# Folding the first layer normalisation into the projection weights, with the x statistics taken late

## The reference

```python
x = x + gnn(layernorm(x), adj, W, a)      # first stage
x = x + ffn(layernorm(x), ...)            # second stage

def layernorm(x): return (x - mean) / sqrt(var + 1e-5)

def gnn(h, adj, W, a):
    Wh = h @ W
    e = (Wh @ a1)[:, :, None] + (Wh @ a2)[:, None, :]
    e = where(e > 0, e, 0.2 * e) + log(adj + 1e-6)
    return softmax(e) @ Wh

def ffn(x, ...):
    w = softmax(mean(x, axis=0) @ Wr + br)       # mean over the 128 graphs
    # per expert: two linear layers with batch norm and relu, one linear layer,
    # weighted by w and summed
```

## Time and profile before

| | us |
|---|---|
| median of 3 runs | 2536.35 (2535.84 to 2540.9) |
| the profiled execution | 2537.31 |
| its span | 2535.5 |
| PE busy | 2412.7 (95%) |
| DVE busy | 1717.1 (68%) |
| ScalarE busy | 1638.9 (65%) |
| POOL busy | 459.4 (18%) |

### The profile page before, as it was taken

How to read it: one execution, slowest core, us unless ns; L and a number is a source line. 1 busy time by engine, 2 the same in 40 slices (tenths; PEclk the granted TensorE clock), 3 DMA queues, 4 the chain that set the end, 5 groups by cost and what they waited for, 6 DMA issues and landing times.

```text
span 2535.5 us, 45093 instructions
## 1 busy us (share of the span) xinstructions
PE 2412.7 (95%) x16304; PEld 2218.3 (87%) x16304; DVE 1717.1 (68%) x2444; ACT 1638.9 (65%) x2497; POOL 459.4 (18%) x487
## 2 busy tenths in 40 slices
PE   6777776999999999999999999999999999999999
PEld 5666665999999999999999999999999999999998
DVE  4777775666666666666666666666666666666665
ACT  4666654666666666666666666666666666666665
POOL 3566553111011111111111111111100111011110
PEclk9999997999999999999999999999999999999999
DMA  3555552000000000000000000000000000000000
GB/s 125 172 186 173 179 165 67 26 20 22 25 17 17 25 25 25 25 25 25 25 25 25 25 25 25 25 25 25 25 25 25 25 24 17 25 17 19 21 17 26
DMA packets 91178, 116.16 MB, mean 46 GB/s; under 512 B 4700, under 2 KB 78856, under 8 KB 91144
## 3 DMA queue, kind: packets, MB, share of 16 engines
q1 hardware_dynamic: 91144, 115.73, 13.9%
HBM read 82.16 MB, written 33.55 MB: 46 GB/s over the span
## 4 chain that ended last, share of the span: by engine, by line
PE 83%; DVE 1%; ACT 0%; issue 0%; ACTq 0%; DVEq 0%
PE ps_y L1182 29%; PE ps_wide L171 28%; PE ps_wide L1164 25%; PE ps_t L132 1%; DVE h_lo L1069 0%; DVE h L1076 0%; PE ps_y L1230 0%; DVE z L1062 0%; DVE x1t L124 0%; ACT h_hi L971 0%; DVE feat_sum L1102 0%; ACT v L976 0%; DVE resb L179 0%; DVE z L1052 0%; DVE h_lo L1084 0%
## 5 line engine op out<-in xcount | busy, mean ns | idle before, releaser
L976 ACT ACTIVATE v<-ps_wide,bn_cols 128x256 f32<-128x256 f32 x768 | 434.3, 566 | 399.3 <-PE ps_wide L1164 269.9
L984 ACT ACTIVATE h<-ps_wide,bn_cols 128x512 f32<-128x512 f32 x512 | 399.0, 779 | 327.5 <-PE ps_wide L171 327.5
L1182 PE MATMUL ps_y<-wo_lo,h_hi 128*128 128x256 f32 x2048 | 579.1, 283 | 0.0
L1182 PE MATMUL ps_y<-wo_hi,h_hi 128*128 128x256 f32 x2048 | 577.4, 282 | 1.6 <-DVE h_lo L1084 1.6
L1182 PE MATMUL ps_y<-wo_hi,h_lo 128*128 128x256 f32 x2048 | 578.6, 283 | 0.0
L1164 PE MATMUL ps_wide<-xq_hi,wq_hi 128*128 128x256 f32 x1792 | 506.2, 282 | 14.9 <-PEq L185 9.2
L1164 PE MATMUL ps_wide<-xq_lo,wq_hi 128*128 128x256 f32 x1792 | 509.7, 284 | 0.0
L1164 PE MATMUL ps_wide<-xq_hi,wq_lo 128*128 128x256 f32 x1792 | 507.1, 283 | 0.0
L1084 DVE TENSOR_TENSOR h_lo<-h,h_hi 128x1024 fp32r<-128x1024 f32 x256 | 318.2, 1243 | 238.9 <-ACT h_hi L990 238.9
L1062 DVE SCALAR_TENSOR_TENSOR z<-ps_wide,bn_cols,v 128x512 f32<-128x512 f32 x256 | 192.2, 751 | 318.0 <-PE ps_wide L1164 318.0
L171 PE MATMUL ps_wide<-h_hi,w_hi 128*128 128x512 f32 x1024 | 404.3, 395 | 2.1 <-DVE h_lo L1069 2.1
(11 more groups left out here) (131 smaller groups left out, 3118.9 us busy)
## 6 DMA issues: line engine op xcount, KB each, us to landing
x_sb<-in_x SPq DMA_DIRECT2D x32, 512.0 KB, 3.9
res<-in_x SPq DMA_DIRECT2D x32, 512.0 KB, 5.8
x1t<-x_scratch SPq DMA_DIRECT2D x32, 512.0 KB, 3.3
resb<-x_scratch SPq DMA_DIRECT2D x32, 512.0 KB, 3.3
out<-resb SPq DMA_DIRECT2D x32, 512.0 KB, 3.0
adj_sb<-in_adj SPq DMA_DIRECT2D x32, 256.0 KB, 6.0
x_scratch<-h SPq DMA_DIRECT2D x16, 512.0 KB, 4.7
x_scratch<-w_bc SPq DMA_DIRECT2D x16, 512.0 KB, 4.5
```

What stands on the lines that cost most here:

```text
L976: nc.scalar.activation(v[:, slot, :], ps_l1[:, 0, 0:H], ACT.Identity, bias=bn_cols[:, 1, cols], scale=bn_cols[:, 0, cols]).then_inc(done, 1)
L984: nc.scalar.activation(h2[:, m, :], ps_l2[:, m, :], ACT.Relu, bias=bn_cols[:, 3, cols], scale=bn_cols[:, 2, cols]).then_inc(r2_done, 1)
L1182: mm = nc.tensor.matmul(ps_y[:, b4, :], h[:, c, cols], w[:, e, c, :], start=(e == 0 and k == 0 and b4 % per_bank == 0), stop=(e == E - 1 a ...
```

## The change

The mean is taken out by the weights: (x - mean) W equals x (W - column mean of W), so at the start two matmuls with a constant matrix of 1/256 (`mean_w`) give the column means and DVE subtracts them from `gw`. The division by the standard deviation is a scale for each row of Wh, and is given to the copy of ps_wide, which becomes one instruction per graph with `rstd1` as its scale. The normalised x isn't written any more: PE transposes `x_sb` itself, and the load of x two groups on waits for those transposes and for the statistics. The statistics of x are needed only by the time of the wh copy, so DVE takes them for g+1, behind the x1 sums, and POOL computes rstd1 behind the running sum. DVE accumulates one graph (`LB = 1`), POOL three. DVE's order in a step changes throughout.

```diff
-                    wait(sp, xn_done, num(g) - 1)
+                    wait(sp, xnT_ready, num(g) - 1)
+                    wait(sp, bnst1, num(g) - 1)
                     sp.dma_start(x_sb[p][:, :, :], x_g[num(g)]).then_inc(x_loaded[p], 16)
...
                 def rstd_1(g):
                     p = g[1]
                     pool.wait_ge(stats1_done, num(g) + 1)
-                    wait(pool, nb1_done, num(g))
-                    nc.gpsimd.tensor_tensor(ve1[:, :], mv1[p][:, :, 1], eps_cols[:, :], ALU.add)
-                    nc.gpsimd.tensor_tensor(neg_mean1[:, :], mv1[p][:, :, 0], minus_one[:, :],
-                                            ALU.mult).then_inc(ve1_done, 1)
+                    wait(pool, rstd1_done, num(g))
+                    nc.gpsimd.tensor_tensor(ve1[:, :], mv1[p][:, :, 1], eps_cols[:, :],
+                                            ALU.add).then_inc(ve1_done, 1)
                     pool.wait_ge(ve1_done, num(g) + 1)
+                    wait(pool, wh_copied, num(g) - 1)
...
-                nxt = ago(g, -2)
-                    if exists(nxt):
-                        rstd_1(nxt)
...
-                        nc.gpsimd.tensor_tensor(acc[:, HB:, :], acc[:, HB:, :], x1s_high[:, :, :],
+                        nc.gpsimd.tensor_tensor(acc[:, LB:, :], acc[:, LB:, :], x1s_high[:, :, :],
                                                 ALU.add).then_inc(acc_high_done, 1)
+                    nxt = ago(g, -1)
+                    if exists(nxt):
+                        rstd_1(nxt)
...
-                    for b4 in range(GB):
-                        last = nc.scalar.activation(xn[:, b4, :], x_sb[p][:, b4, :], ACT.Identity,
-                                                    bias=nb1[p][:, b4:b4 + 1], scale=rstd1[p][:, b4:b4 + 1])
-                    last.then_inc(xn_done, 1)
...
+                        act.wait_ge(rstd1_done, num(g) + 1)
                         wait(act, h_ready, num(g) - 1)
-                        nc.scalar.activation(wh[p][:, :, :], ps_wide[:, :, 0:D + 2], ACT.Copy).then_inc(wh_copied, 1)
+                        for b4 in range(GB):
+                            last = nc.scalar.activation(wh[p][:, b4, :], ps_wide[:, b4, 0:D + 2], ACT.Copy,
+                                                        scale=rstd1[p][:, b4:b4 + 1])
+                        last.then_inc(wh_copied, 1)
...
+                nc.vector.tensor_tensor(gw[:, :, 0:D], gw[:, :, 0:D], ps_wide[:, 0:1, 0:D].to_broadcast([P, C, D]),
+                                        ALU.subtract).then_inc(gw_centred, 1)
...
+                    if exists(nxt):
+                        wait(dve, rstd1_done, num(nxt) - 1)
+                        stats_1(nxt, 0)
+                        stats_1(nxt, 1)
                     if exists(a):
                         dve.wait_ge(e_done, num(a) + 1)
...
+                for c in range(C):
+                    last = nc.tensor.matmul(ps_wide[:, 0, 0:D], mean_w[:, :], gw[:, c, 0:D], start=(c == 0),
+                                            stop=(c == C - 1))
+                last.then_inc(col_mean_ready, 1)
+                pe.wait_ge(gw_centred, 1)
...
-                        pe.wait_ge(xn_done, num(nxt) + 1)
+                        pe.wait_ge(x_loaded[nxt[1]], 16 * (nxt[0] + 1))
...
-                                                           xn[:, b4, c * P:(c + 1) * P], ident[:, :])
+                                                           x_sb[nxt[1]][:, b4, c * P:(c + 1) * P], ident[:, :])
```

More of the change, by code:

```diff
@@ L299, in over_groups @@
             def over_groups(eng, step):
-                for i in range(-2, 2 * K0):
+                for i in range(-1, 2 * K0):
                     step((i // 2, i % 2), 0)
@@ L591, in aggregate_2, with add_part @@
                     last.then_inc(stats2_done, 1)
+                dve.wait_ge(col_mean_ready, 1)
+                nc.vector.tensor_tensor(gw[:, :, 0:D], gw[:, :, 0:D], ps_wide[:, 0:1, 0:D].to_broadcast([P, C, D]),
+                                        ALU.subtract).then_inc(gw_centred, 1)
                 def step(g, layer):
-                    p = g[1]
                     a = ago(g, 1)
+                    b = ago(g, 2)
+                    t = ago(g, 3)
+                    h = ago(g, 4)
                     r = a[1]
-                    nxt = ago(g, -2)
-                    def stats_part(b4):
-                        if exists(nxt):
-                            stats_1(nxt, b4)
+                    q = b[1]
+                    nxt = ago(g, -1)
+                    with_acc = exists(h) and not is_step(h, G - 2) and not is_step(h, G - 1)
+                    with_stats = exists(b) and not is_step(b, G - 1)
+                    def add_part(b4):
+                        if not with_acc or b4 >= LB:
+                            return
+                        if b4 == 0:
+                            dve.wait_ge(rstd2_done, num(h) + 1)
+                            dve.wait_ge(acc_low_done, num(h) + 1)
+                            dve.wait_ge(mean2_done, num(h) + 1)
+                        part = nc.vector.scalar_tensor_tensor(out=acc[:, b4, :], in0=x1[h[1]][:, b4, :],
+                                                              scalar=rstd_all[:, num(h), b4:b4 + 1],
+                                                              in1=acc[:, b4, :], op0=ALU.mult, op1=ALU.add)
+                        if b4 == LB - 1:
+                            part.then_inc(acc_low_done, 1)
+                    if exists(b):
+                        dve.wait_ge(rowsum_done, num(b) + 1)
+                    if exists(t):
+                        dve.wait_ge(bnst2, num(t) + 1)
                     if exists(a):
-                        stats_part(0)
                         dve.wait_ge(s_done, num(a) + 1)
@@ L611, in step @@
                                                        op1=ALU.max).then_inc(l_done, 1)
-                        stats_part(1)
+                    if exists(b):
+                        nc.vector.reciprocal(rinv[:, :], rowsum[:, :]).then_inc(rinv_done, 1)
+                    if exists(t):
+                        aggregate_2(t)
+                    add_part(0)
+                    if exists(a):
                         dve.wait_ge(l_done, num(a) + 1)
@@ L669, in step @@
                         last.then_inc(x1_done, 1)
-                    with_stats = exists(b) and not is_step(b, G - 1)
+                    if exists(nxt):
+                        wait(dve, rstd1_done, num(nxt) - 1)
+                        stats_1(nxt, 0)
+                        stats_1(nxt, 1)
                     if exists(a):
                         dve.wait_ge(e_done, num(a) + 1)
-                        if with_stats:
-                            stats_2(b, 0)
                         dve.wait_ge(adj_loaded[r], 16 * (a[0] + 1))
@@ L681, in step @@
                                                        op1=ALU.mult).then_inc(p_done, 1)
-                        if with_stats:
-                            stats_2(b, 1)
+                    if exists(nxt):
+                        stats_1(nxt, 2)
+                        stats_1(nxt, 3)
+                    if with_stats:
+                        stats_2(b, 0)
+                    if exists(nxt):
+                        dve.wait_ge(bnst1, num(nxt) + 1)
+                    if exists(a):
                         dve.wait_ge(p_done, num(a) + 1)
@@ L686, in step @@
                         nc.vector.tensor_reduce(rowsum[:, :], p_sb[:, :, :], AX_X, ALU.add).then_inc(rowsum_done, 1)
+                    if exists(nxt):
+                        aggregate_1(nxt)
                     if with_stats:
-                        for b4 in range(2 if exists(a) else 0, GB):
+                        for b4 in range(1, GB):
                             stats_2(b, b4)
```

64 lines of the change are left out of this document (13 added, 51 removed).

## The result

The changed kernel took 2514.85 us (median of four runs, 2514.15 to 2515.95), the kernel before 2536.19 beside it. The ratio is 0.9912, 95% interval 0.9895 to 0.9929: faster by 0.9%, 21 us. The direction is as forecast, the size isn't: 2529 was predicted, and the range ended at 2517.

The account below looks back on a forecast made before the run. A loop of waits in the first stage was taken as the bound: 31 x 10.48 = 324.9, + 4.3 + 7.2 = 336.4 against 344.4, so -8.0, + 1.0 = -7.0 us, giving 2529 against the 2536.35 median; range 2517 to 2541.

Parts of the forecast that it names:

- W: Time of ScalarE's four scaled wh copies in one step: forecast 1.55 us, bounds 1.18 and 1.96.
- The loop: First-stage cycle wh, ps_s, s_sb, xnT, projection, ps_h matmuls, next wh: 10.48 us a step after the change, from 10.82.
- The wait for x beside the loop: DVE's wait for x_sb, 2.15 us in one step, was held to be no gain in itself.
- POOL's hold on DVE: While POOL runs, DVE instructions with two SBUF inputs slow: l_sb takes 2.39 us beside wq_lo, its like 0.68.
- So res becomes a new wait of DVE, 1.2 us: In each step res lands 10.8 us after a wh start; the x1 sums would start at 9.56.
- The eight steps with wq_lo (4.3): DVE's accumulation waits behind POOL's wq_lo, delaying wh by 0.54 us in eight steps: 4.3 us.
- My 21.5 for wh: When wh starts in a step with wq_lo: 21.5 us, not the 20.96 due after two intervals.
- The six clock falls (7.2): PE's clock falls in six of the longer-waiting steps, slowing ps_s and transposes by 1.2 us each: 7.2 us.
- a choice between none and one in every step: No row shows PE's single pause of 1.70 us, so its falls were priced between these two extremes.
- Start: Column-mean matmuls and subtraction ahead of the first transposes, 2.7 us in place of the first xn: +0.5 us.
- End: p_sb held by POOL's longer multiply at the end: +0.5 us.
- neither the hold nor falls: Rival: res lands a microsecond sooner, accumulation precedes wq_lo, one or two falls; -17 us, 2519; chance 0.13.

Follow-up runs that it names:

- experiment 5: Changed kernel with a second pointer operand, a zero bias, on each of the four wh copies: 2537.00 us, ratio 0.9996.
- experiment 7: Changed kernel with wh copied by one unscaled instruction, the division by the standard deviation left out: 2506.43 us, ratio 0.9876.
- experiment 2: Kernel before, with the x statistics taken from the always-present gwT so DVE doesn't wait for x: 2534.56 us, ratio 0.9987.
- experiment 8: Changed kernel with PE's transposes of x put ahead of ps_s and ScalarE's xnT ahead of s_sb: 2485.01 us, ratio 0.9790.
- Experiment 6: Changed kernel with SP issuing the res load one step later: 2538.12 us, ratio 1.0002.
- experiment 3: Changed kernel with the x statistics taken two groups ahead, at the head of DVE's step: 2567.35 us, ratio 1.0119.

## Why the prediction was wrong

**What held.** W: 1.57 against 1.55; experiments 5 and 7 give 0.37 more and 0.54 less in W, and 0.38 more and 0.54 less in the loop. An estimate from the figures of the Trainium skill (ScalarE: Activation LUTs, What ACT_TABLE_LOAD costs) was 1.70; the row of s_sb was the better guide. The loop: 10.51 against 10.48, and link by link in the step shown no start is more than 0.05 off. The wait for x beside the loop: experiment 2. POOL's hold on DVE: 2.32 for the accumulation beside wq_lo. The Trainium skill (GPSIMD Engine Reference, Specifications and Key points) names for it instructions with two SBUF inputs, beside those in a 2-port perf mode, and the trace agrees: the x1 sums, one input from PSUM, take 1.66 at 229.55 though POOL's multiply starts at 229.42, while p_sb takes 2.06 in experiment 8.

**The step that failed** is "So res becomes a new wait of DVE, 1.2 us". The issue at 3.8 + 1.2 (5.1 to 5.4 measured in most steps) and the 5.8 to land are nearly right; what they were set against isn't. The x load that SP issues behind the transposes of x(g) is that of step g of its own program, but PE takes those transposes in its step g-1. The res that follows it in the queue is for group g-1, and DVE adds it at the end of the next interval, not of this one. In numbers, from the timeline of SP in the changed kernel and the landing of its res loads (us, min/median/max):

```profile
214.51 0.38 SPq L353 DMA_DIRECT2D res<-in_x  x1
```

```profile
DMA to landing us min/median/max: 4.4/5.7/6.6
```

That load lands at about 220.2, and the sums that use it start at 229.55, 9.3 later. It is 1.2 too late only for the sums one step ahead, and those are the ones in my working. Experiment 6 puts the load where the working had it, and the wait is there, at 1.9 instead of 1.2. Even with it the forecast would have been 7 us too low.

**What hung on it.** The eight steps with wq_lo (4.3): DVE's chain now starts 1.2 sooner, with PE at 9.56. My 21.5 for wh becomes 20.3, inside the 20.96. Measured in the step shown: neg_m ends at 228.58, the exponentials at 229.90, and wh has 0.17 to spare. That the spare is so small is shown by experiment 7. The six clock falls (7.2) were put in the steps that would wait longer, with a pause of 2.2. Those steps are no longer than the others, so the pause stays at 1.75, and no fall comes. The link from pause to fall was not wrong: at 2.03 and 2.11 there are eight (experiment 5). But that 1.7 brings no fall was a choice between none and one in every step, and came true without a row that said so. Two readings behind it were also off. The work around the one pause isn't unbroken, since PE waits 0.83 for xnT in each step. And ahead of the eight falls of before the pause for wh wasn't always about 1.2: it was 1.43 three times and 2.22 once.

**Mis-sized terms.** Start: +0.5 was forecast, and the first projection does start 0.4 later (16.32 against 15.95). But the first wh comes 1.1 earlier, since that projection ran in 5.23 instead of 6.71. The change isn't shown to be the cause: experiment 6 has the same instructions within 0.1 us of the same times up to there, and its first projection takes 6.68; over all the runs it is 5.2 to 6.7. The granted clock reads 1.00 there in either case, so it doesn't explain it. These 1.5 us are luck as far as is known. The first interval: my sum took 31 full ones, but the first has no ps_h matmuls and lasts 8.73, 1.75 less. (The 344.4 of before, from which the gain was taken, held the same short first one, 10.16 in place of 11.1.) End: +0.5 forecast, -0.3 measured.

**The account.** The forecast for the profiled execution was 2530.3, and it took 2514.15. In that difference of 16.2: hold 4.3, falls 7.2, start and first interval 1.6 + 1.75, end 0.8, the second stage 1.4, less 30 x 0.03 for the loop: 16.2. The rival "neither the hold nor falls" was the right case (2519), though not for the reason that it gave: res didn't land sooner, it wasn't wanted yet. The second stage's 1.4 us all lie in its first 36: the first matmul of the experts' third layer (into `ps_y`) starts 35.2 behind the stage's first one, where before it was 36.6. In both kernels the granted clock is below 1.00 there (0.59 and 0.83 in the first two stretches of 20 us, before 0.76 and 0.72). What makes the difference stays open.

## What to carry to other kernels

When a load's landing is set against its use, write out the step numbers of the issuing queue, of the engine that lets the issue go, and of the reader, each in its own program; an offset of one step is ten microseconds here, and decides whether there is a wait at all. Look then at what was hung on that wait, since one wrong wait carried 11.5 us of further terms. And when an experiment brings such a wait back, measure how late its reader starts, not how long the engine stood idle.

Removing work from a loop gives only what it does not uncover: four xn of 2.06 gave 0.31, because ps_s and s_sb stepped into their place. The larger gain, 45 us, came from asking which of the remaining links no longer need each other, moving both ends of that link (on PE alone it gave nothing), and then taking what no one waits for out of the way of neg_m.

## What the runs showed of the hardware

- In this loop a pause of PE of 1.66 to 1.75 us ahead of ps_s in each step, with one of 0.83 ahead of the projection, left the granted clock at 1.00 in all 31 intervals. 2.03 to 2.11 in place of the 1.7 brought it down in eight of 31, mostly 2.3 to 3.2 in 18 (experiment 3). Two pauses of 1.18 and 0.80 around 1.16 us of work, with 0.68 ahead of the projection, as before the change, brought it down in eight too. Filling a part of the first with identity transposes left three.
- A scaled copy of 128x258 from PSUM with one pointer takes 476 ns, with a bias pointer as well 566, and one unscaled copy of all 1032 columns 1030.
- POOL's hold can be hidden or dear in the same instruction: 2.32 against 0.45 for the accumulation cost nothing in a loop of 10.5, while in one of 9.98 the steps with a wq_lo were up to 0.8 longer.
